# First attention of a two-layer decoder: its input load moved inside, the rotation's halves exchanged by ScalarE, four projection banks, the last turning between output products

## The chip, the cores and the metric

The kernel runs as one program on one core of a Trainium2 chip. Its five engines run side by side: TensorE (PE, whose weight loads are listed as PEld), VectorE (DVE), ScalarE (ACT), GpSimd (POOL) and SyncE (SP, which here only issues transfers). They synchronise through semaphores that the program waits for and raises by hand. The metric is the device time of the whole program in microseconds (us), the median of several executions; lower is better.

## The reference, cut to what matters

The model has two layers. Only the first step of the first layer is touched: attention over 4 sequences of 256 tokens and 256 features, with 16 query heads in 4 groups, each group sharing one key and one value head of 128 features.

```
q = jnp.dot(x, q_kernel).reshape(Bs, Ts, K, Gn, H)
k = jnp.dot(x, k_kernel).reshape(Bs, Ts, K, H)
v = jnp.dot(x, v_kernel).reshape(Bs, Ts, K, H)
...
q = (q * qcos + _rotate_half(q) * qsin).astype(q.dtype)
k = (k * kcos + _rotate_half(k) * ksin).astype(k.dtype)
...
for i in range(Gn):
    qi = q[:, :, :, i] * scale
    logits = jnp.einsum('BTKH,BSKH->BKTS', qi, k)
    logits = jnp.tanh(logits / SOFTCAP) * SOFTCAP
    logits = jnp.where(mask, logits, neg)
    probs = jax.nn.softmax(logits.astype(jnp.float32), axis=-1).astype(logits.dtype)
    encoded.append(jnp.einsum('BKTS,BSKH->BTKH', probs, v))
...
return jnp.dot(encoded, out_kernel)
```

`_rotate_half` swaps the two halves of 64 features of a head and negates one of them. The result is added to x. Behind it come, unchanged, a cross attention with layer norms, a mixture of experts, a second layer with a gated delta rule, a latent attention and another mixture.

## The kernel before

**Layout.** x lies in SBUF as 8 tiles of 128 tokens, and turned as `xT` (features on partitions, 2 x 128 features by 1024 tokens). A block of constants (`const`, 128 x 4365 numbers, 2182 KB) holds the identity `ident` for transposes, the tables `a_cos` and `a_sin` of the rotation (512 columns each), the mask `a_mask`, and tables of later stages.

**Input load (`load_inputs`, L149).** A program of its own: SP issues one transfer of x and one of the whole of `const`; PE waits for both (L168), makes 16 transposes of 128 x 128 into PSUM (`turn_x`, L182), and DVE copies them to `xT` in four pieces (L171). A barrier of all engines ends it, and only then does the next program begin.

**First attention (`window_attention`, L186).** A loop over the 4 groups g. SP loads the weights of a group (L219 to L221) as soon as all projections of the group before are done, and the output weights (L223) once its output products are done. Within a group:

1. *Projections.* 10 chunks n of 128 features by 512 tokens (2 of the key, 8 of the four query heads), 2 matmuls each (4 in the trace, since each f32 matmul stands there twice), into the two banks of `pj` in turn (L242). `bank_free` (L231) lets chunk n overwrite chunk n-2 when DVE has done that one's last multiply.
2. *Rotation.* For each chunk DVE makes three multiplies out of PSUM: by the cosine (L304), and two of 64 partitions by the sine that also exchange the halves (L305, L306). GpSimd adds the two results into `qkT` (L330).
3. *Values.* 16 groups of matmuls into both banks of `pj` (L249), which DVE copies to `v` (L310).
4. *Units.* For 16 units u (sequence b, head i): logits on PE (L257, L258) into bank u%2 of `lg`, tanh (L342) and exp (L345) on ACT, the mask's multiply on GpSimd (L334), the product with v on PE into `pv` (L267 to L269, two units behind the logits), division by the row sums on DVE (L314, L317), and for each pair j of units four transposes on PE into `po` (L278, `turn(j)`), which ACT copies to `encT` (L351).
5. *Output.* 8 tiles t of 8 matmuls each into `po` (L293), each added to x by DVE (L320). The loop over units ends with `turn(7)`, and all output products wait until its copy is done:

```
                    for u in range(UN + 3):
                        ...
                        if u >= 4 and u % 2 == 0:
                            turn((u - 4) // 2)
                    pe.wait_ge(wo_loaded, g * 16 + 16)
                    pe.wait_ge(enc_copied, done(g, UN // 2, UN // 2))
                    for t in range(TILES):
```

Semaphores count upward over all groups; `done(g, per, n)` is the value that says that n of this group's `per` steps are done. Every engine works through its own queue strictly in the order of the code, which is written out by hand.

## Time and profile before

| | |
|---|---|
| median of 3 runs | 1599.18 us (1598.6 to 1601.16) |
| the profiled execution's own time | 1597.62 us |
| its span in the trace | 1595.7 us |
| granted PE clock, mean over the span | 0.904 of full speed |
| input load, from the start of the span to the first projection | 22.06 us |
| first attention, from there to the next program's first transfer | 22.06 to 298.16 us |

The span is the time between the first and the last instruction of the trace. The first attention and the load before it are 298 us of it; the 1297 us behind them belong to programs that the change does not touch. The four groups are alike: the value projections of group 0 start at 45.46 us and those of group 3 at 250.04 us, so one group takes 68.2 us.

### The profile page before, as it was taken

How to read it: one execution, taken by the hardware profiler on the slowest of the kernel's cores; microseconds unless marked ns; L12 is line 12 of the kernel's file. 1: busy time of each engine (PE TensorE's matmuls, PEld its weight loads, DVE VectorE, ACT ScalarE, POOL GpSimd, SP SyncE). 2: the span in 40 equal slices, each digit the busy share in tenths (PEclk: the TensorE clock that was granted, in tenths of full speed). 3: DMA queues.
4: the chain of work that ended last, by engine and by line, in shares of the span. 5: the costliest groups of instructions: out<-in, count | busy, mean ns of one | idle time of the engine just before them, and what ended most of it. 6: DMA issues, size and time to landing. Idle time of an engine off the chain costs nothing. (4 is left out here: it accounts for less than half of the span.)

```text
span 1595.7 us, 24725 instructions
## 1 busy us (share of the span) xinstructions
PE 1301.9 (82%) x9098; PEld 838.1 (53%) x9098; DVE 847.9 (53%) x1857; ACT 495.8 (31%) x1157; POOL 515.3 (32%) x596
## 2 busy tenths in 40 slices
PE   5999999832691787999999875788888887999998
PEld 2758577521351454666676763344444444444477
DVE  4463645347139566676764345556554565373334
ACT  0505224120022576666664311233333333100000
POOL 1533526141642467546753112211111111050000
PEclk9999999856795798999999777999999998999999
DMA  3000100490485202212211102000002000554100
GB/s 115 21 16 17 33 13 0 172 273 8 126 224 172 70 14 41 32 29 35 35 24 23 23 0 53 23 24 24 24 24 62 22 1 1 165 178 128 51 4 23
DMA packets 168742, 92.66 MB, mean 58 GB/s; under 512 B 91392, under 2 KB 161768, under 8 KB 168512
## 3 DMA queue, kind: packets, MB, share of 16 engines
q1 hardware_dynamic: 160912, 76.65, 18.2%
q0 software_dynamic: 4496, 13.33, 2.8%
q10 hardware_dynamic: 3232, 1.31, 0.3%
q8 instruction: 65, 1.06, 0.3%
q14 instruction: 37, 0.30, 0.1%
HBM read 76.82 MB, written 15.79 MB: 58 GB/s over the span
## 5 line engine op out<-in xcount | busy, mean ns | idle before, releaser
L2615 PE MATMUL la_banks<-la_xe,la_f_w 128*128 128x512 f32 x348 | 151.4, 593 | 3.4 <-DVE la_xe L3017 3.4
L1933 DVE SCALAR_TENSOR_TENSOR dh_front<-dh_pj,df_conv,dh_front 128x510 f32<-128x510 f32 x144 | 107.4, 746 | 73.2 <-ACT dh_front L1673 69.5
L3181 POOL TENSOR_TENSOR la_area<-la_area 128x512 f32<-128x512 f32 x48 | 60.4, 1273 | 259.1 <-DVE la_area L2874 196.3
L2615 PEld LDWEIGHTS la_banks<-la_xe,la_f_w 128*128 128x128 f32 x348 | 65.4, 190 | 83.6 <-issue 83.5
L2748 ACT ACTIVATE la_area<-la_banks,la_nmax 128x256 f32<-128x256 f32 x128 | 58.9, 472 | 144.4 <-DVE la_nmax L2883 144.4
L2410 PE MATMUL la_banks<-xT,la_area 128*128 128x512 f32 x192 | 91.7, 604 | 1.0 <-ACT la_area L2732 1.0
L330 POOL TENSOR_TENSOR wa_qkT<-wa_t_cos,wa_t_sin 128x512 f32<-128x512 f32 x40 | 50.8, 1270 | 123.8 <-DVE wa_t_sin L306 123.8
L3017 DVE TENSOR_TENSOR la_xe<-xT,la_area 128x1024 f32<-128x1024 f32 x29 | 52.5, 1827 | 55.5 <-PE la_banks L2615 48.1
L342 ACT ACTIVATE wa_capped<-wa_lg 128x384 f32<-128x384 f32 x64 | 31.2, 488 | 161.3 <-PE wa_lg L258 159.9
L2452 PE MATMUL la_banks<-const,la_area 128*128 128x128 f32 x256 | 41.5, 289 | 45.6 <-DVE la_area L2894 30.1
L334 POOL TENSOR_TENSOR wa_masked<-wa_probs,const 128x384 f32<-128x384 f32 x64 | 63.8, 1000 | 40.7 <-ACT wa_probs L345 40.7
L2452 PEld LDWEIGHTS la_banks<-const,la_area 128*128 128x128 f32 x256 | 29.1, 144 | 76.7 <-DVE la_area L2894 41.0
L242 PE MATMUL wa_pj<-xT,wa_wq 128*128 128x512 f32 x128 | 63.5, 618 | 7.1 <-DVE wa_t_sin L306 7.1
L2422 PE MATMUL la_banks<-la_area 128*128 128x512 f32 x96 | 56.7, 738 | 3.6 <-POOL la_area L3181 3.5
L3201 POOL TENSOR_TENSOR la_o_rstd<-la_o_var,la_minus_half 128x1 f32<-128x1 f32 x8 | 6.4, 803 | 164.3 <-DVE la_o_var L3079 164.3
L293 PE MATMUL wa_po<-wa_wo,wa_encT 128*128 128x256 f32 x256 | 56.3, 381 | 3.0 <-ACT wa_encT L351 3.0
L2668 PE MATMUL la_banks<-la_y,la_area 128*128 128x256 f32 x256 | 56.2, 379 | 0.0
L1387 PE MATMUL dh_pj<-xT,df_w 128*128 128x512 f32 x96 | 53.2, 683 | 2.8 <-PEq L133 2.8
L2894 DVE TENSOR_SCALAR la_area<-la_area,la_rec 128x256 f32<-128x256 f32 x128 | 53.4, 479 | 1.1
L293 PEld LDWEIGHTS wa_po<-wa_wo,wa_encT 128*128 128x128 f32 x256 | 48.3, 190 | 10.3 <-issue 3.9
L2668 PEld LDWEIGHTS la_banks<-la_y,la_area 128*128 128x128 f32 x256 | 48.4, 190 | 6.9 <-issue 0.5
L2410 PEld LDWEIGHTS la_banks<-xT,la_area 128*128 128x128 f32 x192 | 33.6, 190 | 34.9 <-issue 32.8
(551 smaller groups left out, 3007.4 us busy)
## 6 DMA issues: line engine op xcount, KB each, us to landing
placed<-mw_rows SPq DMA_DIRECT2D x8, 768.0 KB, 7.8
mw_gu<-in_L_ffn_w_gate SPq DMA_DIRECT2D x16, 384.0 KB
mw_gu<-in_L_ffn_w_up SPq DMA_DIRECT2D x16, 384.0 KB
mw_d<-in_L_ffn_w_down SPq DMA_DIRECT2D x16, 384.0 KB, 7.7
mw_rows<-placed SPq DMA_DIRECT2D x8, 768.0 KB, 5.3
la_area<-w_table POOLq DMA_DIRECT2D x6, 1024.0 KB, 11.6
la_f_w<-in_L_ffn_q_proj SPq DMA_DIRECT2D x32, 128.0 KB, 2.2
la_f_w<-in_L_ffn_k_proj SPq DMA_DIRECT2D x32, 128.0 KB, 2.4
```

The lines of the kernel that those rows point to most:

```text
L242: mm = pe.matmul(pj[:, n % 2, :], w, env.xT[:, k, 512 * c:512 * c + 512], start=(k == 0), stop=(k == KC - 1))
L293: mm = pe.matmul(po[:, t % 2, 0:DIM], encT[:, i, P * t:P * t + P], wos[:, i, :], start=(i == 0), stop=(i == A_G - 1))
L334: pool.tensor_tensor(masked[:, u % 3, :], probs[:, u % 2, :], env.c("a_mask"), ALU.mult).then_inc(mask_done, 1)
L1933: dve.scalar_tensor_tensor(dst, src[:, :, 0:SEQ - j], conv[:, a, m, D_CONV - 1 - j:D_CONV - j], dst, ALU.mult, ALU.add).then_inc(tapped, 1)
L2410: mm = pe.matmul(qb[:, n, :], wabs[:, k, n, :], env.xT[:, k, 512 * c:512 * c + 512], start=(k == 0), stop=(k == KC - 1))
L2422: mm = pe.matmul(po, mabs[:, n, :], qrot[:, c, n, :], start=(n == 0), stop=(n == 2))
L2452: mm = pe.transpose(tr[turn_bank(j, a)][:, P * (2 * l + n):P * (2 * l + n) + P], en[:, u % 2, a, n, P * l:P * l + P], env.c("ident"))
L2615: mm = pe.matmul(acc[c][m], f_w[n % SLOTS][:, m, k, :], xe[(n - U) % RING][:, k, :], start=first and k == 0, stop=last and k == KC - 1)
L2668: mm = pe.matmul(o_acc[t % 4], ae[t % RING][:, x, :], f_wo[:, x, :], start=(x == 0), stop=(x == F_E - 1))
L2748: ins = act.activation(e[:, u % 2, a, n, :], sc[bank(j, b)][:, a, n, :], ACT.Exp, bias=nmax[:, a, t:t + 1], accum_out=total[:, a, t:t + 1])
L2894: ins = dve.tensor_scalar(en[:, u % 2, a, n, :], e[:, u % 2, a, n, :], rec[:, a, 2 * b + n:2 * b + n + 1], None, ALU.mult)
L3181: pool.tensor_tensor(qrot[:, c, n, :], prod[:, c, 2 * n, :], prod[:, c, 2 * n + 1, :], ALU.add).then_inc(rotated, 1)
```

## The change

- `load_inputs` and `turn_x` are gone. x comes in two transfers from SP and `const` in three from ScalarE's queue: `ident`, then the tables and the mask, then the rest, which is issued behind ACT's copies and waited for only at the end of the attention. For that the columns of `const` are reordered. The 16 transposes go into `pv` and `po`; DVE copies the low half of the features of each token half, ACT the high half.
- The exchange of the halves in the rotation is done by two copies of 64 partitions on ScalarE, from PSUM to the new tile `swap`; DVE then makes two multiplies of 128 partitions, one from PSUM and one from `swap`. The sign in `a_sin` is mirrored.
- The chunks of the projections use four banks (`q_bank`: two of `pj`, two of `pv`).
- The logits of units 0 and 1 stand ahead of the value projections.
- Output products 0 and 1 stand ahead of the last turning, which goes into bank 0 of `lg`.

The diff, cut to its core:

```diff
-    with ExitStack() as ctx:
-        sb, ps, sem = tools(nc, ctx, "load")
...
-                sp.dma_start(env.x[:], x_in.rearrange("b (u p) c -> p (b u) c", p=P)).then_inc(loaded, 16)
-                sp.dma_start(env.const[:], const_in).then_inc(loaded, 16)
...
+        q_bank = [pj[:, 0, :], pj[:, 1, :], pv[:, 0, :], pv[:, 1, :]]
+        x_tp = [(pv[:, 0, :], pv[:, 1, :]), (po[:, 0, :], po[:, 1, :])]
...
+                for th in range(2):
+                    sp.dma_start(env.x[:, 4 * th:4 * th + 4, :], rows[:, 4 * th:4 * th + 4, :]).then_inc(x_loaded[th], 16)
...
+                pe.wait_ge(ident_loaded, 16)
+                for th in range(2):
+                    pe.wait_ge(x_loaded[th], 16)
+                    for k in range(KC):
+                        for j in range(4):
+                            mm = pe.transpose(x_tp[th][k][:, P * j:P * j + P], env.x[:, 4 * th + j, P * k:P * k + P], env.c("ident"))
+                        mm.then_inc(x_turned, 1)
...
                         if n < 2:
                             pe.wait_ge(v_copied, done(g, 2, n - 1))
+                            pe.wait_ge(x_low, n + 1)
+                            pe.wait_ge(x_high, n + 1)
+                        elif n < 4:
+                            pe.wait_ge(normed, done(g, UN, 0))
                         else:
-                            pe.wait_ge(sin_done, done(g, 2 * QCH, 2 * (n - 1)))
+                            last = n - 3 if n < QCH else n - 1
+                            pe.wait_ge(cos_done, done(g, QCH, last))
+                            pe.wait_ge(swapped, done(g, 2 * QCH, 2 * last))
...
+                    def output(t):
+                        if t == 0:
+                            pe.wait_ge(wo_loaded, g * 16 + 16)
+                            pe.wait_ge(enc_copied, done(g, TURNS, TURNS - 2))
+                        elif t == 1:
+                            pe.wait_ge(enc_copied, done(g, TURNS, TURNS - 1))
+                        elif t == 6:
+                            pe.wait_ge(enc_copied, done(g, TURNS, TURNS))
...
+                    output(0)
+                    output(1)
+                    turn(TURNS - 1)
+                    for t in range(2, TILES):
+                        output(t)
...
-                        dve.tensor_tensor(t_cos[:, n % 2, :], pj[:, n % 2, :], env.c("a_cos"), ALU.mult).then_inc(cos_done, 1)
-                        dve.tensor_tensor(t_sin[0:HALF, n % 2, :], pj[HALF:P, n % 2, :], env.c("a_sin")[HALF:P, :], ALU.mult).then_inc(sin_done, 1)
-                        dve.tensor_tensor(t_sin[HALF:P, n % 2, :], pj[0:HALF, n % 2, :], env.c("a_sin")[0:HALF, :], ALU.mult).then_inc(sin_done, 1)
+                        dve.wait_ge(swapped, done(g, 2 * QCH, 2 * n + 2))
+                        dve.tensor_tensor(t_cos[:, n % 2, :], q_bank[n % 4], env.c("a_cos"), ALU.mult).then_inc(cos_done, 1)
+                        dve.tensor_tensor(t_sin[:, n % 2, :], swap[:, n % 2, :], env.c("a_sin"), ALU.mult).then_inc(sin_done, 1)
...
+                def swap_halves(g, n):
+                    act.wait_ge(projected, done(g, PJ, n + 1))
+                    act.wait_ge(sin_done, done(g, QCH, n - 1))
+                    act.copy(swap[0:HALF, n % 2, :], q_bank[n % 4][HALF:P, :]).then_inc(swapped, 1)
+                    act.copy(swap[HALF:P, n % 2, :], q_bank[n % 4][0:HALF, :]).then_inc(swapped, 1)
```

How it moves instructions. First PE's queue at the end of a group. In the kernel before, the rows from the product of unit 15 (L267 to L269 there) over the last turning (L278) to the first two output products (L293) are:

```order
L267 MATMUL wa_pv<-wa_v,wa_masked 128x129 [waits wa_normed,wa_mask_done]
L268 MATMUL wa_pv<-wa_v,wa_masked 128x129
L269 MATMUL wa_pv<-wa_v,wa_masked 128x129
L276 REGISTER_ALU [waits wa_normed]
L278 MATMUL wa_po<-const,wa_enc 128x128 [waits wa_enc_copied]
L278 MATMUL wa_po<-const,wa_enc 128x128 x3
L291 REGISTER_ALU [waits wa_enc_copied]
L293 MATMUL wa_po<-wa_wo,wa_encT 128x256 [waits wa_added]
L293 MATMUL wa_po<-wa_wo,wa_encT 128x256 x3
```

After the change the same place reads (L240 to L242 is the product, L267 now an output product, L254 a turning):

```order
L240 MATMUL wa_pv<-wa_v,wa_masked 128x129 [waits wa_normed,wa_mask_done]
L241 MATMUL wa_pv<-wa_v,wa_masked 128x129
L242 MATMUL wa_pv<-wa_v,wa_masked 128x129
L265 REGISTER_ALU [waits wa_enc_copied]
L267 MATMUL wa_po<-wa_wo,wa_encT 128x256 [waits wa_added]
L267 MATMUL wa_po<-wa_wo,wa_encT 128x256 x3
L262 REGISTER_ALU
L267 MATMUL wa_po<-wa_wo,wa_encT 128x256 [waits wa_added,wa_enc_copied]
L267 MATMUL wa_po<-wa_wo,wa_encT 128x256 x3
L254 MATMUL wa_lg<-const,wa_enc 128x128 [waits wa_capped_done,wa_normed]
L254 MATMUL wa_lg<-const,wa_enc 128x128 x3
```

Two tiles of output products now stand between the last product of the units and the last turning, and the turning writes to `lg`.

Second, DVE's queue at a chunk of the projections. In the kernel before one chunk is:

```order
L303 ISA [waits load_copied]
L304 TENSOR_TENSOR wa_t_cos<-wa_pj,const 128x512 [waits wa_rotated]
L305 TENSOR_TENSOR wa_t_sin<-wa_pj,const 64x512
L306 TENSOR_TENSOR wa_t_sin<-wa_pj,const 64x512
L302 REGISTER_ALU
```

(The name `load_copied` in the first row stands for a semaphore whose number `projected` uses again.) After it:

```order
L309 ISA [waits wa_projected]
L310 ISA [waits wa_swapped]
L311 TENSOR_TENSOR wa_t_cos<-wa_pj,const 128x512 [waits wa_rotated]
L312 TENSOR_TENSOR wa_t_sin<-wa_swap,const 128x512
L308 REGISTER_ALU
```

One multiply fewer, a wait for ScalarE more, and the sine's multiply reads both its inputs from SBUF.

Third, ScalarE's queue from its start, where the program of before had only the table load ahead of the first tanh. Now:

```order
L367 DMA const<-in_const 128x128
L368 DMA const<-in_const 128x1408
L371 ACT_TABLE_LOAD
L371 COPY xT<-wa_pv 128x512 [waits wa_x_turned]
L371 COPY xT<-wa_po 128x512 [waits wa_x_turned]
L372 DMA const<-in_const 128x2829
L373 UNCONDITIONAL_BRANCH
L373 ISA
L349 ISA [waits wa_projected]
L350 COPY wa_swap<-wa_pj 64x512 [waits wa_sin_done]
L351 COPY wa_swap<-wa_pj 64x512
```

Ten such pairs of copies stand in each group ahead of its first tanh (L355 now), and the table load has left the loop.

## Rows read from the trace of the kernel before

**Rows 1.** The page's first part: busy time, share of the span and instructions

```profile
PE 1301.9 (82%) x9098; PEld 838.1 (53%) x9098; DVE 847.9 (53%) x1857; ACT 495.8 (31%) x1157; POOL 515.3 (32%) x596
```

**Rows 2.** Timeline, first 30 us: start, duration, engine, line, operation [idle before <- releaser]

```profile
0.76 0.44 SPq L158 DMA_DIRECT2D x<-in_x  x1
...
11.73 3.68 PE L182 MATMUL load_tp<-const,x 128*128 128x128 f32 x16 [11.73 <-DMA const<-in_const]
...
15.45 0.69 DVE L171 COPY xT<-load_tp 128x512 f32<-128x512 f32 x1 [0.16 <-PE load_tp L182]
...
17.16 0.41 SPq L219 DMA_DIRECT2D wa_wq<-in_L_attn_q_kernel  x1
...
22.06 5.85 PE L242 MATMUL wa_pj<-xT,wa_wk 128*128 128x512 f32 x8 [6.66 <-DMA wa_wv<-in_L_attn_v_kernel]
```

**Rows 3.** Windows of the load: stretch, its length, busy us by engine, PEclk, DMA share, GB/s

```profile
2.00:4.00 2.00, 0.00 (x0) 0.00 (x0) 0.00 (x0) 0.00 (x0) 0.00 (x0) 1.00 0.80 227
4.00:10.00 6.00, 0.00 (x0) 0.00 (x0) 0.00 (x0) 0.00 (x0) 0.00 (x0) 1.00 1.07 437
...
20.00:22.00 2.00, 0.00 (x0) 0.00 (x0) 0.00 (x0) 0.00 (x0) 0.00 (x0) 1.00 1.03 331
```

**Rows 4.** Timeline of one chunk of group 1's projections

```profile
107.14 0.69 DVE L304 TENSOR_TENSOR wa_t_cos<-wa_pj,const 128x512 f32<-128x512 f32 x1
107.16 1.98 PE L242 MATMUL wa_pj<-xT,wa_wq 128*128 128x512 f32 x4 [0.18 <-DVE wa_t_sin L306]
107.19 1.27 POOL L330 TENSOR_TENSOR wa_qkT<-wa_t_cos,wa_t_sin 128x512 f32<-128x512 f32 x1 [0.89 <-DVE wa_t_sin L306]
...
108.59 0.68 DVE L306 TENSOR_TENSOR wa_t_sin<-wa_pj,const 64x512 f32<-64x512 f32 x1
109.30 0.69 DVE L304 TENSOR_TENSOR wa_t_cos<-wa_pj,const 128x512 f32<-128x512 f32 x1
```

**Rows 5.** Timeline of group 1: first chunk, DVE's answer, value projections, first weighted product

```profile
92.15 3.60 PE L242 MATMUL wa_pj<-xT,wa_wk 128*128 128x512 f32 x8
...
94.17 0.69 DVE L304 TENSOR_TENSOR wa_t_cos<-wa_pj,const 128x512 f32<-128x512 f32 x1 [1.39 <-PE wa_pj L242]
...
113.65 4.21 PE L249 MATMUL wa_pj<-wa_wv,xT 128*128 128x128 f32 x32 [0.18 <-DVE wa_t_sin L306]
117.70 0.60 PE L257 MATMUL wa_lg<-wa_qkT 128*128 128x256 f32 x2
...
120.96 0.48 PE L267 MATMUL wa_pv<-wa_v,wa_masked 128*128 128x129 f32 x2 [0.87 <-POOL wa_masked L334]
```

**Rows 6.** Lines, shapes kept apart: operations of known cost, xcount | busy us, mean ns

```profile
L334 POOL TENSOR_TENSOR wa_masked<-wa_probs,const 128x384 f32<-128x384 f32 x64 | 63.8, 1000 | 40.7 <-ACT wa_probs L345 40.7
...
L1729 ACT COPY dh_TT<-dh_lv 64x512 f32<-64x512 f32 x11 | 6.4, 578 | 11.7 <-PE dh_lv L1483 11.7
...
L452 ACT ACTIVATE xc_kvT<-xc_kp,xc_b 64x512 f32<-64x512 f32 x2 | 1.4, 682 | 22.5 <-PE xc_kp L405 22.5
```

**Rows 7.** Timeline in the experts' routing: DVE with two SBUF inputs beside POOL

```profile
365.65 0.69 DVE L899 TENSOR_TENSOR me_cand<-me_scb,me_gm 128x512 f32<-128x512 f32 x1
365.76 3.37 POOL L1036 TENSOR_TENSOR me_s_u<-me_s_h,me_s_u 96x512 f32<-96x512 f32 x2 [13.48 <-ACT me_s_u L821]
366.38 1.64 DVE L900 TENSOR_TENSOR me_cand<-me_cand,me_gpen 128x512 f32<-128x512 f32 x1
```

**Rows 8.** Timeline of group 3's end: last product, last turning, its copy, output

```profile
280.23 0.39 PE L269 MATMUL wa_pv<-wa_v,wa_masked 128*128 128x129 f32 x2
281.41 0.65 PE L278 MATMUL wa_po<-const,wa_enc 128*128 128x128 f32 x4 [0.80 <-DVE wa_enc L317]
282.82 14.08 PE L293 MATMUL wa_po<-wa_wo,wa_encT 128*128 128x256 f32 x64 [0.75 <-ACT wa_encT L351]
...
282.10 0.59 ACT L351 COPY wa_encT<-wa_po 128x512 f32<-128x512 f32 x1 [1.89 <-PE wa_po L278]
```

**Rows 9.** Windows of the attention and of a stretch behind it

```profile
22.00:298.00 276.00, 256.23 (x1312) 188.14 (x1312) 139.91 (x288) 86.54 (x163) 114.60 (x104) 1.00 0.05 16
...
320.00:400.00 80.00, 22.19 (x75) 14.24 (x75) 48.53 (x163) 15.23 (x33) 24.09 (x30) 0.59 0.52 138
```

More of the change, by code:

```diff
@@ L54, in constants @@
     parts["ident"] = (row == col)
-    parts["ones"] = np.ones((P, P))
-    parts["upto"] = (row <= col)
-    parts["after"] = (row > col)
-    parts["before"] = (row < col)
     frac = (np.arange(0, A_HD, 2, dtype=f) / f(A_HD)).astype(f)
@@ L62, in constants @@
     ang = (np.arange(SEQ, dtype=f)[None, :] * np.concatenate([inv, inv])[:, None]).astype(f)
-    sign = np.where(row < P // 2, 1.0, -1.0)
+    sign = np.where(row < P // 2, -1.0, 1.0)
     parts["a_cos"] = np.tile(np.cos(ang), (1, 2))
@@ L69, in constants @@
     parts["a_mask"] = np.concatenate([m0, (row <= col)], 1)
+    parts["ones"] = np.ones((P, P))
+    parts["upto"] = (row <= col)
+    parts["after"] = (row > col)
+    parts["before"] = (row < col)
     parts["m_head"] = (row // 32 == np.arange(4)[None, :])
@@ L146, in tools, with window_attention @@
     return sb, ps, sem
[L149 to L186 removed]
+def window_attention(nc, env, x_in, const_in, wq, wk, wv, wo):
     SCALE = float(A_HD) ** -0.5
@@ L197, in window_attention @@
     UN = BATCH * A_G
+    TURNS = UN // 2
+    START = sum(env.at[n][1] for n in ("ident", "a_cos", "a_sin", "a_mask"))
     with ExitStack() as ctx:
@@ L274, in turn @@
                             pe.wait_ge(added, done(g, TILES, 0))
-                        else:
-                            pe.wait_ge(enc_copied, done(g, UN // 2, j - 1))
+                        elif j == TURNS - 1:
+                            pe.wait_ge(capped_done, done(g, UN, UN))
+                        else:
+                            pe.wait_ge(enc_copied, done(g, TURNS, j - 1))
+                        bank = lg[:, 0, :] if j == TURNS - 1 else po[:, j % 2, :]
                         for n in range(4):
-                            mm = pe.transpose(po[:, j % 2, P * n:P * n + P], enc[:, (2 * j + n // 2) % 4, n % 2, :], env.c("ident"))
+                            mm = pe.transpose(bank[:, P * n:P * n + P], enc[:, (2 * j + n // 2) % 4, n % 2, :], env.c("ident"))
@@ L279, in turn @@
                         mm.then_inc(turned, 1)
-                    for u in range(UN + 3):
+                    def output(t):
[6 more added lines that the diff above has]
+                            pe.wait_ge(enc_copied, done(g, TURNS, TURNS))
+                        pe.wait_ge(added, done(g, TILES, t - 1))
+                        for i in range(A_G):
+                            mm = pe.matmul(po[:, (t + 1) % 2, 0:DIM], encT[:, i, P * t:P * t + P], wos[:, i, :], start=(i == 0), stop=(i == A_G - 1))
+                        mm.then_inc(out_done, 1)
@@ new lines, in _ @@
+                    for n in range(QCH):
+                        m, c = divmod(n, CH)
+                        bank_free(n)
+                        for k in range(KC):
+                            w = wks[:, k, :] if m == 0 else wqs[:, k, A_HD * (m - 1):A_HD * m]
+                            mm = pe.matmul(q_bank[n % 4], w, env.xT[:, k, 512 * c:512 * c + 512], start=(k == 0), stop=(k == KC - 1))
+                        mm.then_inc(projected, 1)
+                    logits(0)
+                    logits(1)
@@ L282, in _ @@
+                    for h in range(2):
+                        bank_free(QCH + h)
+                        for j in range(4):
+                            t = 4 * h + j
+                            for k in range(KC):
+                                mm = pe.matmul(pj[:, h, P * j:P * j + P], env.xT[:, k, P * t:P * t + P], wvs[:, k, :], start=(k == 0), stop=(k == KC - 1))
+                        mm.then_inc(projected, 1)
+                    for u in range(2, UN + 2):
                         if u < UN:
@@ L283, in _ @@
                             logits(u)
-                        if 2 <= u < UN + 2:
-                            weighted(u - 2)
+                        weighted(u - 2)
                         if u >= 4 and u % 2 == 0:
                             turn((u - 4) // 2)
-                    pe.wait_ge(wo_loaded, g * 16 + 16)
-                    pe.wait_ge(enc_copied, done(g, UN // 2, UN // 2))
-                    for t in range(TILES):
-                        pe.wait_ge(added, done(g, TILES, t - 1))
-                        for i in range(A_G):
-                            mm = pe.matmul(po[:, t % 2, 0:DIM], encT[:, i, P * t:P * t + P], wos[:, i, :], start=(i == 0), stop=(i == A_G - 1))
-                        mm.then_inc(out_done, 1)
+                    output(0)
@@ L299, in _ @@
                 dve.memset(v[:, :, A_HD:A_HD + 1], 1.0)
+                for th in range(2):
+                    dve.wait_ge(x_turned, 2 * th + 1)
+                    dve.tensor_copy(env.xT[:, 0, 512 * th:512 * th + 512], x_tp[th][0]).then_inc(x_low, 1)
+                dve.wait_ge(tables_loaded, 16)
                 with dve.Fori(0, A_KV) as g:
```

78 lines of the change are left out of this document (27 added, 51 removed).

## The prediction

> **What bounds the kernel now.** I read the page first, for one thing only: PE is busy 82% of the span [rows 1], so time comes from places where PE waits, or where it works slower than it can. Then the timeline of the load, since the change rebuilds it. There the reader is to see three waits in a row on one path: PE's first transpose waits until 11.73 us for the transfer of `const`; a barrier follows the last copy of `xT` at 15.45 us, and the weights are not even asked for before 17.16 us; the first projection waits for them until 22.06 us [rows 2]. PE works 3.7 us in these 22.
>
> Next the timeline of one group, read three times. In the projections each chunk takes from one cosine multiply to the next: 109.30 - 107.14 = 2.16 us, and DVE is busy all of it (three multiplies of 0.69 us, 0.72 us from start to start). PE's four matmuls take 1.98 us, but their last one's tail overlaps what follows [rows 4]: in the first two chunks, which find both banks free, 8 of them take 3.60 us [rows 5], and the 64 output matmuls of half the width take 14.08 us, 0.22 us each [rows 8], so a chunk is 4 x 0.43 = 1.73 us of PE. GpSimd's add of 1.27 us has 0.89 us idle ahead of it [rows 4]. DVE sets this stage. Behind it, from the first projection of a group to its first weighted product, 120.96 - 92.15 = 28.81 us pass, of them 3.26 from the first logits to that product, where tanh, exp and mask run one after the other with PE mostly waiting [rows 5]. In the units themselves PE works without a gap, and the change leaves that loop alone. At the end of a group PE has done its last weighted product at 280.23 + 0.22 = 280.45 us, waits 0.80 us for DVE's division ahead of the last turning and 0.75 us for ACT's copy behind it, and the output starts at 282.82 [rows 8].
>
> **The load.** It removes a barrier, a wait for most of `const`, and the order "first all inputs, then the weights". What has to come before the first projection is x (1024 KB), `ident` (64), the tables (704) and three weights (768). DMA moved 227 GB/s from 2 to 4 us, so 0.45 MB, and 437 GB/s from then on [rows 3]. x, `ident` and tables (1792 KB = 1.84 MB) are in at 4 + 1.38/0.437 = 7.2 us. The weights, with shorter pieces, moved at 331 GB/s [rows 3]: 0.79 MB more take 2.4 us, which gives 9.5 us, and with part of the output weights in between and the completion I take 10.3. Bounds: all at 437 gives 9.0 us, all at 331 with the whole of the output weights (0.52 MB) ahead gives 12.1. The transposes cost 3.68/16 = 0.23 us each [rows 2]: the eight of the second half take 1.8 us from 7.2 and the copy 0.7 [rows 2], 9.8 us in all, so they hide behind the weights. Gain 22.06 - 10.3 = **11.8 us** (10.0 to 13.1).
> The first 8 projection matmuls took 5.85 us in group 0 [rows 2] and 3.60 in group 1 [rows 5]: in group 0 PE came out of 6.66 us of idleness and ran at about half pace. Here it idles only 1 to 2 us between transposes and projections. That may give back up to 2.2 us; the nearest row, PE's slow start in spite of 3.7 us of transposes shortly before, shows none, so I take 0. The table load of ACT is covered by the wait for x. The third transfer of `const` (1414 KB) is needed only behind the attention, hundreds of us later: 0.
>
> **The projections, per group.** Each chunk now goes PE, two ACT copies, cosine, sine, add. ACT: the same shape of copy took 0.58 us, with a bias 0.68 [rows 6]; the pair costs 1.25 us, below the 1.73 of PE (1.4 would be too). DVE: two multiplies, 1.44 us. PE: 1.73 us, and with four banks it has no wait on a chunk just done. The question is the pair sine and add. Before, DVE's multiplies had one input in PSUM, and stayed at 0.69 us beside a running add [rows 4]. Now the sine's multiply has two SBUF inputs. In the routing such a multiply, started at 366.38 while GpSimd was in a multiply of two SBUF tiles, took 1.64 us instead of 0.69, and GpSimd's two together took 3.37 us [rows 7], against 1.27 for one [rows 4]. 3.37/2 = 1.68, so the first ended near 367.45, and the DVE instruction ended 366.38 + 1.64 = 368.02, 0.57 us behind that. The two exclude each other and only some 0.12 us overlaps. Here: add n starts 0.08 us behind sine n (107.19 is that far behind 108.59 + 0.68 - 2.16 [rows 4]) and takes 1.27; cosine n+1 runs beside it; sine n+1 is at its turn 0.72 us behind the last, is held until the add ends, and ends 0.57 us later. The chunk's period is 0.08 + 1.27 + 0.57 = **1.92 us**, above PE's 1.73 and below the 2.16 of before.
>
> The Trainium skill, page "SBUF — State Buffer", section "Who interferes with whom", speaks against this edit: a VectorE instruction with two SBUF inputs and a GpSimd instruction that reads SBUF hold a shared port exclusively, and the later one is blocked for the other's whole duration. Taken by the letter, with full durations in a row, the period would be 0.69 + 0.08 + 1.27 = 2.04 us and the sum below 4.3 us smaller; the trace agrees on the exclusion (1.64 us) and shows that a little overlaps.
>
> The path to the first weighted product, from the group's first matmul: 2.02 us until the first chunk is handed over (94.17 - 92.15) [rows 5], 1.25 swap, 1.41 cosine and sine, 1.35 hand-off and add, 9 x 1.92 = 17.3 for the other chunks, 1.0 mask [rows 6], 0.1 hand-off: **24.4 us** against 28.81. Tanh and exp of unit 0 no longer stand in it: the first two logits come ahead of the values, ACT has its last swap behind it around 19.3, and GpSimd reaches the mask only at 23.3. PE is no bound: 10 chunks (17.3), values 4.05 (117.70 - 113.65) and three logits with at most 3.26 - 0.87 = 2.4 make 23.7 [rows 5]; the second half of the values waits for cosine 9 near 20.8 and needs 2.0, which ends at 22.8. Gain 4.4 us per group, **17.6 us**.
>
> **The end of a group.** Output tiles 0 and 1 need turnings 0 and 1 and the bank of turning 6, whose copy is over. They start at 280.45 instead of 282.82; the last turning's four transposes still cost PE 0.43 (0.65 with their tail) [rows 8]. The division of unit 15 and the copy hide behind 1.73 us per output tile. Gain 2.37 - 0.43 = 1.94 us per group, **7.8 us**. If the copy were late, output 6 would wait: it comes four tiles, 6.9 us, later, against 0.59. Moving on to the next group adds no wait: its weights were loaded dozens of us before.
>
> **Sum.** 11.8 + 17.6 + 7.8 = 37.2 us. Against the profiled execution's own 1597.62 us that is 1560.4; the median shown is 1.56 above it, which gives **1562**.
>
> **The rivals.**
> 1. *The hand-off ACT to DVE to GpSimd costs what the third multiply did.* Each chunk now has two more hand-offs, and the lock may cost more than its one sighting here. With a period of 2.16 as before, the path is 26.6 us and the gain 2.2 per group: 1571. For it: there is one clean sighting of the lock. Against: 0.24 us per chunk would have to come on top of a measured 1.64. Chance 17%.
> 2. *No exclusion for this pair.* Then PE sets the pace at 1.73 and the path falls to 22.7, where PE's own work (22.8 to 23.7) takes over: 5.1 to 6.0 per group: 1556 to 1559. Against: [rows 7]. Chance 13%.
> 3. *Later programs meet another clock.* All through the attention the granted clock is 1.00, but from 320 to 400 us it is 0.59 with 22.19 us of PE work [rows 9]. At 0.50 throughout that work takes 4 us more, at 1.00 9 us less, if it is on the path. The stages keep their order, so little should change: 1553 to 1566. Chance 12%.
> 4. *The load does not get earlier as it should*: the two queues share the engines so that the last weight lands with everything else, and projections start near 16: 1568. Against: nothing beyond 3.1 MB is asked for by then. Chance 5%.
> 5. *Slower than before.* The rings do not overlap: `swap`, with two buffers, holds ACT for the sine, which waits for the add, which waits for the sine. The sum turns negative when 11.8 + 7.8 + 4 x (28.81 - 7.1 - 9p) < 0, so at a period p of 2.96 us. Fully in a row a chunk would be 1.25 + 1.41 + 1.35 = 4.0 us, and the time 1599 + 4 x 9 x (4.0 - 2.96) = 1636. Against: two buffers let ACT work one chunk ahead. Chance 3%.
>
> **The numbers.** Forecast 50%, with a range of its own of 1557 to 1567. The range of 8 in 10 takes in rivals 1 to 3 in full and the load's bounds: 1553 to 1573. A change of 0.2% (3.2 us) is about what a measurement of this kernel can tell. Faster by more: 96%; within: 1%; slower: 3%.
>
> **What the profile after would show.** First projection at 10.3 us; sine multiplies (L312) of about 1.2 us instead of 0.69, because a held instruction's wait shows in its duration, cosines still 0.69; GpSimd's adds 1.92 us apart with 0.65 idle between them; 24.4 us from a group's first matmul to its first weighted product; output starting 0.2 us behind unit 15's product and the turning inside it at 0.43; one group 61.9 us instead of 68.2. The forecast is wrong if sines stay at 0.69 us (rival 2), if PE waits on a bank in the projections, or if the programs behind the attention differ by more than 2 us.

## The result and the profile after

The changed kernel takes 1560.06 us (median of 4 executions, 1558.78 to 1563.48) against 1599.18, which is of 4 executions too: ratio 0.9757, interval 0.9739 to 0.9774. The prediction was 1562 with a range of 1553 to 1573. The profiled execution took 1560.39 us, with a span of 1558.6 us. Its first two lines answer to [rows 1]:

```profile
span 1558.6 us, 24915 instructions
...
PE 1295.6 (83%) x9098; PEld 843.0 (54%) x9098; DVE 833.0 (53%) x1815; ACT 540.4 (35%) x1236; POOL 515.3 (33%) x596
```

DVE has 42 instructions fewer: 40 multiplies, and two of the four copies of `xT`. ACT has 82 copies more, two of them for `xT`, and three table loads fewer. ACT is busy 44.6 us longer with them, DVE 14.9 us less and PE 6.3 us less; such totals do not tell where the 37 us come from. These lie in the order of work, which the timeline of the first 25 us begins to show:

```profile
2.12 0.39 SPq L192 DMA_DIRECT2D wa_wk<-in_L_attn_k_kernel  x1
...
5.09 1.94 PE L206 MATMUL wa_pv<-const,x 128*128 128x128 f32 x8 [5.09 <-DMA x<-in_x]
...
8.10 1.97 PE L206 MATMUL wa_po<-const,x 128*128 128x128 f32 x8 [1.07 <-DMA x<-in_x]
...
10.10 0.59 ACT L371 COPY xT<-wa_po 128x512 f32<-128x512 f32 x1 [2.45 <-PE wa_po L206]
...
10.80 5.41 PE L275 MATMUL wa_pj<-xT,wa_wk 128*128 128x512 f32 x8 [0.73 <-ACT xT L371]
...
22.83 0.68 DVE L311 TENSOR_TENSOR wa_t_cos<-wa_pj,const 128x512 f32<-128x512 f32 x1
...
22.99 1.27 POOL L337 TENSOR_TENSOR wa_qkT<-wa_t_cos,wa_t_sin 128x512 f32<-128x512 f32 x1 [0.63 <-DVE wa_t_sin L312]
...
23.43 1.37 DVE L312 TENSOR_TENSOR wa_t_sin<-wa_swap,const 128x512 f32<-128x512 f32 x1
...
24.73 0.68 DVE L311 TENSOR_TENSOR wa_t_cos<-wa_pj,const 128x512 f32<-128x512 f32 x1
...
24.88 1.27 POOL L337 TENSOR_TENSOR wa_qkT<-wa_t_cos,wa_t_sin 128x512 f32<-128x512 f32 x1 [0.63 <-DVE wa_t_sin L312]
```

Against [rows 2], the weights are asked for at 2.12 instead of 17.16 us, and the first projection starts at 10.80 instead of 22.06. Its last releaser is ACT's copy of the high half of `xT`, which hangs on the second half of x at 8.10 us. Against [rows 4], a chunk takes 24.73 - 22.83 = 1.90 us instead of 2.16. The cosine beside the add keeps its 0.68 us. The sine, with both inputs in SBUF, is started during the add and shows 1.37 us: the add ends at 24.26, the sine at 24.80, 0.54 us later. The wait for the add stands inside the DVE instruction's duration, and DVE looks busy while it is held.

PE's timeline of group 1 answers to [rows 5], that of group 3's end to [rows 8]:

```profile
74.09 3.60 PE L275 MATMUL wa_pj<-xT,wa_wk 128*128 128x512 f32 x8
...
91.26 0.59 PE L230 MATMUL wa_lg<-wa_qkT 128*128 128x256 f32 x2
...
92.71 3.95 PE L284 MATMUL wa_pj<-wa_wv,xT 128*128 128x128 f32 x32
...
98.21 0.48 PE L240 MATMUL wa_pv<-wa_v,wa_masked 128*128 128x129 f32 x2 [0.90 <-POOL wa_masked L341]
...
244.02 0.39 PE L242 MATMUL wa_pv<-wa_v,wa_masked 128*128 128x129 f32 x2
244.24 3.62 PE L267 MATMUL wa_po<-wa_wo,wa_encT 128*128 128x256 f32 x16
247.70 0.60 PE L254 MATMUL wa_lg<-const,wa_enc 128*128 128x128 f32 x4
248.13 10.53 PE L267 MATMUL wa_po<-wa_wo,wa_encT 128*128 128x256 f32 x48
```

The first weighted product comes 98.21 - 74.09 = 24.12 us behind the group's first matmul, instead of 28.81. The output starts 0.22 us behind the last product instead of 2.59, and the turning inside it costs 248.13 - 247.70 = 0.43 us.

The same boundaries, read from the PE timelines of all kernels of this study, in us. "Path" is from a group's first matmul to its first weighted product (group 0, then a later group), "units" from there to the first output product, "output" from there to the next group; "next" is the first transfer of the program behind. Kernels are named by their labels' first part:

| kernel | first projection | path | units | output | next |
|---|---|---|---|---|---|
| before | 22.06 | 30.71, 28.81 | 25.47 | 13.91 | 298.16 |
| after | 10.80 | 25.94, 24.12 | 23.10 | 14.25 | 260.00 |
| after, measured again (e10) | 10.87 | 25.82, 24.11 | 23.10 | 14.26 | 259.95 |
| e1 halves into PSUM | 10.89 | 25.72, 23.00 | 23.11 | 14.25 | 256.54 |
| e2 three multiplies | 10.85 | 28.43, 27.76 | 23.11 | 14.25 | 274.77 |
| e3 two banks | 10.82 | 28.66, 26.14 | 23.10 | 14.26 | 268.84 |
| e4 turning first | 10.73 | 26.95, 24.12 | 25.49 | 13.91 | 269.12 |
| e5 old load | 23.57 | 27.30, 25.37 | 23.11 | 14.25 | 277.91 |
| e6 logits behind | 10.97 | 28.15, 25.65 | 23.10 | 14.25 | 266.98 |
| e7 tables later | 9.47 | 26.25, 24.09 | 23.10 | 14.25 | 258.93 |
| e8 e1 and e7 | 10.10 | 23.06, 22.99 | 23.11 | 14.26 | 253.09 |
| e9 e2, values in pv | 10.90 | 27.98, 26.04 | 24.76 | 14.26 | 274.53 |
| e12 e8, key weights apart | 8.70 | 23.27, 23.00 | 23.11 | 14.25 | 251.91 |

The next program starts 298.16 - 260.00 = 38.16 us earlier. Of that the load gives 11.26, the paths 4.77 in group 0 and 4.69 in each of the others, and units with output (25.47 + 13.91) - (23.10 + 14.25) = 2.03 in each group, 38.2 in all. What lies behind takes 1298.6 instead of 1297.5 us, so the span is 37.1 shorter.

That last stretch varies by itself: the changed kernel, measured again (e10), takes 1288.2 us there, and the other kernels, whose programs behind the attention are the same, 1281.9 (e9) to 1307.2 (e6). What makes it vary is not shown. So an edit worth a few microseconds is judged below from the table, and from medians only where they can tell.

### The profile page after: what moved, and what is told of

Same layout as the page of the kernel before. It is cut to its first block and busy times, and to the rows that moved or that the text cites. A ratio compares the mean times of both kernels' runs of the same rounds, so it can differ in the third digit from the quotient of the medians.

```text
span 1558.6 us, 24915 instructions
## 1 busy us (share of the span) xinstructions
PE 1295.6 (83%) x9098; PEld 843.0 (54%) x9098; DVE 833.0 (53%) x1815; ACT 540.4 (35%) x1236; POOL 515.3 (33%) x596
## 5 line engine op out<-in xcount | busy, mean ns | idle before, releaser
L267 PE MATMUL wa_po<-wa_wo,wa_encT 128*128 128x256 f32 x256 | 56.6, 379 | 0.0
L267 PEld LDWEIGHTS wa_po<-wa_wo,wa_encT 128*128 128x128 f32 x256 | 48.0, 190 | 6.2
L312 DVE TENSOR_TENSOR wa_t_sin<-wa_swap,const 128x512 f32<-128x512 f32 x40 | 48.4, 1210 | 0.0
L1410 PE MATMUL dh_pj<-xT,dh_w 128*128 128x512 f32 x96 | 48.2, 627 | 0.0
## 6 DMA issues: line engine op xcount, KB each, us to landing
la_area<-w_table POOLq DMA_DIRECT2D x6, 1024.0 KB, 12.8
```

Source lines behind the costliest of these rows:

```text
L267: mm = pe.matmul(po[:, (t + 1) % 2, 0:DIM], encT[:, i, P * t:P * t + P], wos[:, i, :], start=(i == 0), stop=(i == A_G - 1))
L1410: mm = pe.matmul(pj[:, n % 2, :], w[a % 2][:, m, k, :], env.xT[:, k, 512 * s:512 * s + 512], start=(k == 0), stop=(k == KC - 1))
```

## The experiments

e1 to e4, e5 to e8, and e9, e10 and e12 were each measured together on one chip; the kernel before took 1595.53, 1600.5 and 1586.74 us beside them. The ratios below are against these.

**One input of the sine in PSUM (e1).** ACT puts the exchanged halves into the two banks of `po`, which are free in this phase, and the tile `swap` is gone:

```diff
-                        dve.tensor_tensor(t_sin[:, n % 2, :], swap[:, n % 2, :], env.c("a_sin"), ALU.mult).then_inc(sin_done, 1)
+                        dve.tensor_tensor(t_sin[:, n % 2, :], po[:, n % 2, :], env.c("a_sin"), ALU.mult).then_inc(sin_done, 1)
...
+                    if n < 2:
+                        act.wait_ge(added, done(g, TILES, 0))
-                    act.copy(swap[0:HALF, n % 2, :], q_bank[n % 4][HALF:P, :]).then_inc(swapped, 1)
+                    act.copy(po[0:HALF, n % 2, :], q_bank[n % 4][HALF:P, :]).then_inc(swapped, 1)
```

> The changed kernel with one edit: ScalarE writes the exchanged halves into the two banks of po (PSUM) instead of the SBUF tile swap, so the sine's multiply has one SBUF input again. Theory (the multiply with two SBUF inputs and GpSimd's add exclude each other, and that sets the period of 1.90 us): sine 0.69 us instead of 1.21, adds 1.72 us apart (PE's pace), 22.7 to 23.0 us instead of 24.12 from a group's first matmul to its first weighted product, 1.1 to 1.4 us less per group, next program at 254.5 to 255.5 us instead of 260.0, time about 1555. Rival (the 1.90 comes from the hand-offs ACT to DVE to GpSimd, not from a shared port): sine and period as in the changed kernel, time 1560. A third: ScalarE writes PSUM more slowly than SBUF, its pair of copies takes over 1.7 us and becomes the bound: time 1560 or more.

Its timeline in group 1:

```profile
85.46 1.27 POOL L337 TENSOR_TENSOR wa_qkT<-wa_t_cos,wa_t_sin 128x512 f32<-128x512 f32 x1 [0.45 <-DVE wa_t_sin L312]
85.81 0.69 DVE L311 TENSOR_TENSOR wa_t_cos<-wa_pj,const 128x512 f32<-128x512 f32 x1 [0.43 <-ACT wa_po L353]
86.42 0.68 DVE L312 TENSOR_TENSOR wa_t_sin<-wa_po,const 128x512 f32<-128x512 f32 x1
87.18 1.27 POOL L337 TENSOR_TENSOR wa_qkT<-wa_t_cos,wa_t_sin 128x512 f32<-128x512 f32 x1 [0.45 <-DVE wa_t_sin L312]
```

The sine in the view by lines (xcount | busy us, mean ns | idle before):

```profile
L312 DVE TENSOR_TENSOR wa_t_sin<-wa_po,const 128x512 f32<-128x512 f32 x40 | 27.2, 681 | 0.0
```

The same row of the changed kernel:

```profile
L312 DVE TENSOR_TENSOR wa_t_sin<-wa_swap,const 128x512 f32<-128x512 f32 x40 | 48.4, 1210 | 0.0
```

The sine starts at 86.42 while the add runs until 86.73 and still takes 0.68 us: only where the other input lies has changed, so the exclusion between a DVE multiply of two SBUF tiles and GpSimd's add is shown. The period falls to 1.72 us, and DVE now waits 0.43 us for ACT in each chunk: PE, with 1.72 for four matmuls, has become the bound. The path falls by 1.12 us in groups 1 to 3, but only by 0.22 in group 0, where the first eight matmuls took 6.32 us instead of 5.41. So the next program comes 3.46 us earlier, less than the 4.5 to 5.5 expected. The median, 1559.98 us (ratio 0.9781, 0.9746 to 0.9816), can't show that.

**No exchange by ACT: three multiplies on DVE, with four banks (e2).**

```diff
-                            pe.wait_ge(cos_done, done(g, QCH, last))
-                            pe.wait_ge(swapped, done(g, 2 * QCH, 2 * last))
+                            pe.wait_ge(sin_done, done(g, 2 * QCH, 2 * last))
...
-                        dve.tensor_tensor(t_sin[:, n % 2, :], swap[:, n % 2, :], env.c("a_sin"), ALU.mult).then_inc(sin_done, 1)
+                        dve.tensor_tensor(t_sin[0:HALF, n % 2, :], q_bank[n % 4][HALF:P, :], env.c("a_sin")[HALF:P, :], ALU.mult).then_inc(sin_done, 1)
+                        dve.tensor_tensor(t_sin[HALF:P, n % 2, :], q_bank[n % 4][0:HALF, :], env.c("a_sin")[0:HALF, :], ALU.mult).then_inc(sin_done, 1)
```

> The changed kernel without its exchange by ScalarE: DVE makes three multiplies out of PSUM again, with four banks and everything else as changed. Theory: period 2.16 us (DVE), but no swap in the first chunk's path: 2.0 + 2.1 + 1.35 + 9 x 2.16 + 1.1 = 26.0 us against 24.1 to the first weighted product, +1.9 us per group, +7.6 in all: about 1568. Rival (the exchange is worth all of the 4.7 us that this stretch lost): 28.8 us, +18.8 in all: about 1579.

The path is 27.76 us, in group 1 even 29.02, and the time 1570.94 us (ratio 0.9866, 0.9816 to 0.9917). The timeline of group 1 shows PE waiting ahead of the values, and then slow:

```profile
98.15 6.73 PE L283 MATMUL wa_pj<-wa_wv,xT 128*128 128x128 f32 x32 [2.87 <-DVE wa_t_sin L311]
...
105.67 0.49 PE L239 MATMUL wa_pv<-wa_v,wa_masked 128*128 128x129 f32 x2
```

The window of these values shows the clock (its length, busy us of PE, PEld, DVE, ACT and POOL, PEclk, DMA share, GB/s):

```profile
98.15:104.70 6.55, 6.55 (x32) 6.55 (x33) 2.74 (x4) 0.00 (x0) 4.46 (x4) 0.53 0.00 0
```

With two banks PE waited 0.18 us ahead of each chunk and of the values [rows 4, 5]. With four it runs ahead of DVE, and then waits 2.87 us in one piece for the sines that read the banks of the values. Behind that wait the granted clock is 0.53, close to the lower of its two levels, 1.2 GHz. The values take 6.57 us (98.15 to the next row of PE at 104.72) instead of 3.78 (92.71 to 96.49). In group 2 they take 5.30, at a granted clock of 0.68; in group 0, behind a wait of 2.41, they take 4.05. So my 26.0 had left out PE's slower pace behind the wait, if nothing else is hidden there; e9 tests that.

**The same, with the values in the banks of pv (e9, profiled once).** This takes away PE's wait ahead of the values (DVE's copies to `v` and PE's waits for the banks follow the edit):

```diff
-                                mm = pe.matmul(pj[:, h, P * j:P * j + P], env.xT[:, k, P * t:P * t + P], wvs[:, k, :], start=(k == 0), stop=(k == KC - 1))
+                                mm = pe.matmul(pv[:, h, P * j:P * j + P], env.xT[:, k, P * t:P * t + P], wvs[:, k, :], start=(k == 0), stop=(k == KC - 1))
```

> The kernel of e2 (three multiplies by DVE) with one more edit: the values are projected into the banks of pv, which chunks 6 and 7 have left, instead of pj, which DVE still reads for chunks 8 and 9. In e2 a group took 27.8 to 29.0 us to its first weighted product where 26.0 were expected; there PE waited 2.87 us for the sine multiplies ahead of the values and then did them in 5.5 to 6.7 us instead of 3.95. Theory (the missing 1.8 to 3 us are this wait for the banks and PE's slower pace behind it): no wait, values in 3.7 to 4.0 us, first weighted product at 26.0 to 26.3 us, next program near 268. Rival (the third multiply itself costs it, by way of GpSimd's adds): 27.8 or more as in e2, next program near 274.

The path is 26.04 us, but the units take 24.76 instead of 23.10. PE's timeline:

```profile
96.37 3.74 PE L283 MATMUL wa_pv<-wa_wv,xT 128*128 128x128 f32 x32
...
103.93 0.48 PE L239 MATMUL wa_pv<-wa_v,wa_masked 128*128 128x129 f32 x2 [3.17 <-POOL wa_masked L340]
104.25 0.56 PE L240 MATMUL wa_pv<-wa_v,wa_masked 128*128 128x129 f32 x2
```

And a window behind PE's new wait:

```profile
104.00:107.00 3.00, 3.00 (x14) 2.82 (x15) 0.60 (x2) 0.86 (x2) 1.71 (x2) 0.55 0.25 84
```

The values are back at 3.7 us and the path at the 26.0 that I had for e2. Now PE waits 3.17 us for the mask instead, the clock is 0.55 behind that, and the next program starts at 274.53, as in e2 (274.77). The chain DVE to GpSimd to mask is too long; PE's idle time only moves along it, and the lower clock moves with it. The exchange by ACT is therefore worth 274.77 - 260.00 = 14.8 us here, not four times (26.0 - 24.12) = 7.5: it also keeps PE from that wait.

**Two banks (e3).** `q_bank` is the two banks of `pj`, and chunk n waits for cosine and exchange of chunk n-2:

```diff
-        q_bank = [pj[:, 0, :], pj[:, 1, :], pv[:, 0, :], pv[:, 1, :]]
+        q_bank = [pj[:, 0, :], pj[:, 1, :]]
...
-                            last = n - 3 if n < QCH else n - 1
+                            last = n - 1
```

> The changed kernel with the projections in the two banks of pj alone. Theory: a chunk's matmuls now wait for the cosine two chunks before: two chunks take 2.0 + 1.25 + 0.7 = 4.0 us, so the period is 2.0 us instead of 1.90, +1.0 us per group, +4 in all: about 1564. Rival (GpSimd and the sine set 1.90 anyway, banks are no bound): within 1 us of the changed kernel. Second rival (four banks carry the gain): period 2.5 or more, +5 per group, 1580.

```profile
80.97 3.69 PE L273 MATMUL wa_pj<-xT,wa_wq 128*128 128x512 f32 x8 [0.53 <-DVE wa_t_cos L309]
...
83.06 0.58 ACT L348 COPY wa_swap<-wa_pj 64x512 f32<-64x512 f32 x1 [1.33 <-PE wa_pj L273]
83.66 0.58 ACT L349 COPY wa_swap<-wa_pj 64x512 f32<-64x512 f32 x1
84.36 0.69 DVE L309 TENSOR_TENSOR wa_t_cos<-wa_pj,const 128x512 f32<-128x512 f32 x1 [1.03 <-ACT wa_swap L349]
...
85.18 3.70 PE L273 MATMUL wa_pj<-xT,wa_wq 128*128 128x512 f32 x8 [0.52 <-DVE wa_t_cos L309]
```

Two chunks take 85.18 - 80.97 = 4.21 us, all in a ring: matmuls and hand-off until 83.06 (2.09), the copies until the cosine (1.30), cosine and hand-off (0.82). That is 2.11 per chunk, 0.21 above the changed kernel's; over nine chunks 1.9, and measured +2.02 per group, twice what I had expected. The next program comes 8.84 us later (1570.61 us, ratio 0.9835, 0.9789 to 0.9881).

**The last turning ahead of all output products (e4).** The order is that of before; unlike there, and unlike what the expectation says, the turning still goes into `lg`:

```diff
-                    output(0)
-                    output(1)
                     turn(TURNS - 1)
-                    for t in range(2, TILES):
+                    pe.wait_ge(enc_copied, done(g, TURNS, TURNS))
+                    for t in range(TILES):
                         output(t)
```

> The changed kernel with its last turning ahead of all output products and into po again, and the output waiting for its copy. Theory: the two waits of 0.80 and 0.75 us come back with the time around them, 2.0 us per group, +8.1 in all: about 1568. Rival: DVE and ACT have become freer and the waits are shorter than before, under +4.

```profile
251.10 0.39 PE L242 MATMUL wa_pv<-wa_v,wa_masked 128*128 128x129 f32 x2
252.21 0.65 PE L254 MATMUL wa_lg<-const,wa_enc 128*128 128x128 f32 x4 [0.72 <-DVE wa_enc L322]
```

PE waits 0.72 us for DVE's division again, and the output follows at 253.71, 2.61 us behind the last product (2.59 before), so the bank of the turning has no part in it. Units and output together take 25.49 + 13.91 = 39.40 us instead of 37.35: +2.05 per group. Group 0's path is 1.01 longer too: its first eight matmuls took 6.62 us instead of 5.41, and the edit has no part in these. The next program comes 9.1 us later; 1571.48 us (ratio 0.9857, 0.9817 to 0.9897).

**The load as a program of its own (e5):** the old `load_inputs` and `turn_x` ahead of an attention that is otherwise the changed one.

```diff
+        load_inputs(nc, env, a["x"], a["const"])
...
-                act.dma_start(env.const[:, 0:P], const_in[:, 0:P]).then_inc(ident_loaded, 16)
-                act.dma_start(env.const[:, P:START], const_in[:, P:START]).then_inc(tables_loaded, 16)
-                for th in range(2):
-                    act.wait_ge(x_turned, 2 * th + 2)
-                    act.copy(env.xT[:, 1, 512 * th:512 * th + 512], x_tp[th][1]).then_inc(x_high, 1)
-                act.dma_start(env.const[:, START:], const_in[:, START:]).then_inc(rest_loaded, 16)
                 with act.Fori(0, A_KV) as g:
```

> The changed kernel with the input load of before as a program of its own ahead of it (x and the whole of const first, then the transposes, a barrier, then the weights). Theory: the first projection returns from 10.80 to about 22 us and nothing else changes: +11.3 us, about 1571. Rival (part of the load's gain is taken back inside group 0, because PE runs slower there in the changed kernel): less than +9.

The first projection starts at 23.57 us, 12.8 later. That is 1.5 us behind the 22.06 of before, though the weights are asked for at the same time; why is not shown. And the paths are 1.36 us longer in group 0 and 1.25 in the others, which no theory had:

```profile
90.21 1.28 ACT L370 ACT_TABLE_LOAD   x1 [11.56 <-PE wa_pj L300]
91.50 0.58 ACT L370 COPY wa_swap<-wa_pj 64x512 f32<-64x512 f32 x1
...
92.81 0.69 DVE L332 TENSOR_TENSOR wa_t_cos<-wa_pj,const 128x512 f32<-128x512 f32 x1 [3.97 <-ACT wa_swap L371]
```

Without ACT's copies of `xT` ahead of the loop, the table load stands inside it again, once per group. It starts only when the first chunk is there, and the exchange waits for it. Before the change it was there too, four times at L342, but ahead of the first tanh. There it ran as soon as ACT was done with the group before, and ACT was idle for 39.15 us behind it, so it cost nothing. From the kernel before:

```profile
78.13 1.28 ACT L342 ACT_TABLE_LOAD   x1
118.56 0.49 ACT L342 ACTIVATE wa_capped<-wa_lg 128x384 f32<-128x384 f32 x1 [39.15 <-PE wa_lg L258]
```

So the new load program does two things: it starts the projections earlier, and it takes the table load out of a loop where the exchange has made it expensive. The next program comes 17.9 us later (12.8 + 1.36 + 3 x 1.25); 1573.94 us (ratio 0.9846, 0.981 to 0.9883).

**Logits 0 and 1 behind the values (e6).**

```diff
-                    logits(0)
-                    logits(1)
                     for h in range(2):
...
+                    logits(0)
+                    logits(1)
```

> The changed kernel with the logits of units 0 and 1 behind the value projections again. Theory: the values end 22.2 us behind a group's first matmul, then logits, tanh, exp and mask follow one another for 3.0 us: first weighted product at 25.3 to 25.5 instead of 24.1, +1.2 to 1.4 per group, about 1565. Rival (GpSimd's adds set the mask's time, whatever the order): within 1 us.

```profile
98.22 1.27 POOL L337 TENSOR_TENSOR wa_qkT<-wa_t_cos,wa_t_sin 128x512 f32<-128x512 f32 x1 [0.63 <-DVE wa_t_sin L312]
...
98.86 0.60 PE L230 MATMUL wa_lg<-wa_qkT 128*128 128x256 f32 x2
...
99.72 0.49 ACT L355 ACTIVATE wa_capped<-wa_lg 128x384 f32<-128x384 f32 x1 [4.15 <-PE wa_lg L231]
...
101.00 2.97 POOL L341 TENSOR_TENSOR wa_masked<-wa_probs,const 128x384 f32<-128x384 f32 x3 [1.51 <-ACT wa_probs L358]
...
102.12 0.48 PE L240 MATMUL wa_pv<-wa_v,wa_masked 128*128 128x129 f32 x2 [0.87 <-POOL wa_masked L341]
```

GpSimd, done with its adds at 99.49, waits 1.51 us for tanh and exp; ACT was idle for 4.15. The path is +1.53 per group, close to what was expected; next +7.0; 1571.32 us (ratio 0.9811, 0.9776 to 0.9845).

**The tables' transfer behind ACT's first copy (e7),** so that x and the weights have the DMA engines to themselves, **and together with e1 (e8):**

```diff
-                act.dma_start(env.const[:, P:START], const_in[:, P:START]).then_inc(tables_loaded, 16)
                 for th in range(2):
...
+                    if th == 0:
+                        act.dma_start(env.const[:, P:START], const_in[:, P:START]).then_inc(tables_loaded, 16)
```

> The changed kernel with the second transfer of constants (tables and mask, 704 KB) issued by ScalarE behind its first copy of xT instead of at the start. Theory (the load is bound by bytes that need not come first): second half of x at about 6.3 us instead of 8.1, weights at 8.5 to 9, first projection at about 9 us instead of 10.80, the tables still in time: 1.5 to 2 us less, about 1558. Rival (they come too late for the first cosine at 15.9 us, or the weights' own short pieces set the time): no gain or a loss.

> Both edits together: the exchanged halves in PSUM and the tables' transfer later. If both theories hold the gains add: 5 + 1.8 us, about 1553. If either falls, what is left is the other's.

PE's timelines of e7 and of e8:

```profile
9.47 5.93 PE L275 MATMUL wa_pj<-xT,wa_wk 128*128 128x512 f32 x8 [0.53 <-DMA wa_wv<-in_L_attn_v_kernel]
```

```profile
10.10 3.67 PE L275 MATMUL wa_pj<-xT,wa_wk 128*128 128x512 f32 x8 [1.47 <-DMA wa_wv<-in_L_attn_v_kernel]
```

In e7 the second half of x is there in time, and the projections start 1.33 us earlier, released by the last weight. Their first eight matmuls take 0.52 longer, group 0's path 0.31, and the next program gains 1.07. In e8 the same edit gives a start at 10.10, 0.63 later than in e7 for the same transfers (why is not shown), but those matmuls at full pace, 3.67 us; with e1's gain the next program comes 6.9 us earlier. Medians: 1561.09 (0.9743, 0.9706 to 0.9781) and 1554.89 us (0.9703, 0.9653 to 0.9753).

**A wait of its own for the key weights (e12),** on top of e8, beside the changed kernel again (e10). PE waits for the first weight's transfer alone before chunk 0. Its edit beside those of e8:

```diff
-                    pe.wait_ge(w_loaded, g * 48 + 48)
+                    pe.wait_ge(wk_loaded, g * 16 + 16)
...
+                        if n == CH:
+                            pe.wait_ge(w_loaded, g * 32 + 32)
```

> The changed kernel itself, unedited, for a comparison on one chip with the kernel of e12. All theories: next program at 260 us (give or take 1 us for PE's pace in group 0), the time 1560 with whatever the programs behind it add: in the nine profiles so far the rest of the span took 1292 to 1307 us.

> The kernel of e8 (exchanged halves in PSUM, the tables' transfer later) with the wait for the weights split: the first two chunks wait for the key weights alone, the third for the rest. Theory: the key weights land near 7 us, so the first projection comes right behind the last transpose, at 8.6 to 8.9 us instead of 9.5 to 10.1, and the second chunk at 9.3; next program at 251.5 to 253.5 us, 7 us less than the changed kernel, time about 1553. Rival (PE works at half pace at first, whenever it starts, so an earlier start is given back inside group 0): next program at 253 to 254.

```profile
6.99 1.92 PE L206 MATMUL wa_po<-const,x 128*128 128x128 f32 x8
...
8.70 3.87 PE L277 MATMUL wa_pj<-xT,wa_wk 128*128 128x512 f32 x8
```

And a window over nearly the whole of the attention:

```profile
10.00:250.00 240.00, 238.80 (x1309) 188.50 (x1309) 108.16 (x247) 127.47 (x240) 114.33 (x104) 1.00 0.08 25
```

The first projection now follows the last transpose without a wait, and the next program starts at 251.91 instead of 259.95. From 10 to 250 us PE is busy 238.80 of 240 us, against 234.99 in the changed kernel. The median is 1539.82 us (ratio 0.9702, 0.968 to 0.9725) against 1550.42 on that chip (0.9755, 0.9724 to 0.9785): the fastest version here, 10.6 us below the changed kernel, of which the attention shows 8.0.

## Why the prediction was right

**The load.** Forecast 10.3 us, measured 10.80. I had x, `ident` and the tables in at 7.2 us, the weights behind them, and the transposes hidden. Instead the second half of x came at 8.10, and the transposes and the copy behind it were last. The weights landed at about the same time: in e2 and e6, whose load is the same, PE is released by `wa_wv` at 10.85 and 10.97. The step that was off is that I let PE start when x's last byte is in. From 2 to 4, 4 to 6 and 6 to 8 us DMA moved 272, 411 and 359 GB/s in the profile after, so some 1.8 MB by 7.2 us, as forecast. But in the kernel before nothing moves any more from 11.0 us on, and PE starts only at 11.73. Some 0.8 us of this kind (my estimate) behind 7.2 gives 8.0, and with transposes and copy 10.6. I had put a completion to the weights, and none to x. How the bytes of x, tables and weights mixed is not shown; that the tables have a share is: with them moved away (e7) PE finds the second half of x there at 7.03 and starts at 9.47. The error is 0.5 us.

**PE's first matmuls.** I took no gain for the pace of the first eight, and they took 5.41 instead of 5.85: 0.44 us, inside the bound of 2.2. They took from 3.67 (e8) to 6.62 us (e4) over the kernels that have the new load, and the edits don't order them; the changed kernel itself took 5.41 and 5.29 (e10). That 0 was nearly right here is luck.

**The period and the lock.** Forecast 1.92 us, measured 1.90, with a sine of 1210 ns in the mean (1.2 forecast) and 0.63 us idle ahead of the add (0.65). The one sighting of the lock [rows 7] had it right to 0.03: there the held multiply ended 0.57 us behind GpSimd's instruction, here 0.54. The Trainium skill, page "SBUF — State Buffer", section "Who interferes with whom", has the later instruction blocked for the whole of the other's. e1 agrees on who excludes whom, down to one PSUM input being enough to be free of it. By the letter the period would have been 2.04; measured is 1.90, so here too about 0.14 us of the held instruction overlaps, and the measurement decides.

**The path.** Forecast 24.4, measured 24.12: nine periods of 0.02 less make 0.2 of it. Group 0 has its own path, 25.94 us, and gained 4.77 only because its path was longer before as well; I had taken all four groups as alike. That the logits hide tanh and exp is shown by e6 (+1.53 without it). That four banks are needed is shown by e3. I had costed them at nothing by themselves; they are worth 2.02 us per group, because a chunk holds its bank through two copies now.

**The end of a group.** Forecast 1.94, measured 2.03, and e4 takes 2.05 back.

**Behind the attention.** +1.06 us between the two profiles, inside the 2 us that I had allowed. But the changed kernel's own two profiles (1298.6 and 1288.2) lie 10 us apart there, more than the 9 us that I had given this rival downwards (1553 against 1562), and e10's median, 1550.42, lies below my whole range; the kernel before took 1586.74 beside it, and the ratio is the same (0.9755). That the sum matched to 2 us is in part luck of the pair of profiles; the 38.16 us up to the next program are not, since the two profiles give 260.00 and 259.95.

**The sum and its parts.** Forecast 11.8 for the load, 17.6 for the paths and 7.8 for the ends of the groups; measured 11.26, 18.84 and 8.1. Taken back one by one, the load (17.9), the exchange (14.8), the turning (9.1), the banks (8.8) and the logits (7.0) make 57.6 us, against the 38.16 of all together. Some of that is chance: in group 0 PE's first matmuls were slower than the changed kernel's in each of these runs, which is 0.7 us in e3 and e6 and 1.0 in e4. The rest overlaps: without one, PE waits in one piece where the others had removed the waits, and pays for it in the clock (e2), or the exchange exposes a table load (e5). None of the rivals holds as it stood: the period is not 2.16 (rival 1), the sine is not free of the lock (rival 2), the programs behind differ by 1.06 us in this pair (rival 3), projections start at 10.80 and not near 16 (rival 4), and the rings overlap (rival 5).

## What to carry to other kernels

Before two engines split elementwise work, look at where each input lies: beside a GpSimd add, one DVE operand in PSUM instead of SBUF took the period of a chunk from 1.90 to 1.72 us, until PE set the pace, and 3.5 us in all. A held instruction counts as busy, so look for a group's mean duration above its usual one, not for idle time. And when one stage is made faster, ask where the idle time of PE collects next: spread over many small waits it costs its own length, but gathered into one of 2.87 or 3.17 us it was followed by slower matmuls here.

## What the runs showed of the hardware

- The granted clock fell to 0.53 and 0.68 behind PE's waits of 2.87 us in groups 1 and 2 of e2, and to 0.55 behind one of 3.17 us in e9. Equal waits had unequal results: groups 1 and 2 of e2 run the same code. Behind 2.41 us, in its group 0, 32 matmuls took 4.05 us.
- In group 0 the records don't carry the pace: the first eight matmuls of the changed kernel take 5.41 us where 3.60 is the rule, while the granted clock reads 1.00 in that window, as it does in e4, where they take 6.62. In e5, where they take 6.47 us, it reads 0.56. Why the records differ is open.
- ACT copies 64x512 from PSUM in 582 ns to SBUF and 558 ns to PSUM (e1). The Trainium skill, page "ScalarE: Activation LUTs", section "Step-by-step: what each stage is for", says that ScalarE writes PSUM faster than SBUF, and this agrees; the gain is 24 ns.
- A table load of 1.28 us stood in the loop in every iteration (e5, before), and outside it when an ACT copy came ahead of the loop (after). It cost nothing where it ran ahead of an idle time of ACT of 39.15 us, and 1.25 us per group where it stood behind the wait for the first chunk.
